# Depthwise 7x7 layer of a four-layer conv kernel: planes in lines of nine values, three window loads per half

## The reference

```python
def _L3_conv_ref(x, w, b):
    xp = jnp.pad(x, ((0, 0), (0, 0), (P, P), (P, P)), mode='reflect')
    out = jax.lax.conv_general_dilated(xp, w, window_strides=(S, S), padding='VALID',
                                       dimension_numbers=('NCHW', 'OIHW', 'NCHW'), feature_group_count=C)
    return out + b[None, :, None, None]
...
x = x + _L3_conv_ref(_gn(x), L3_conv_w, L3_conv_b)
```

## Time and profile before

| | before |
|---|---|
| median of 3 runs | 2541.14 us (2539.9 to 2541.88) |
| the profiled execution's own time | 2520.47 us |
| its span | 2518.7 us |
| mean granted TensorE clock | 0.887 |
| TensorE busy | 1939.4 us (77%) |
| VectorE busy | 1286.7 us (51%) |
| ScalarE busy | 803.1 us (32%) |
| GpSimd busy | 865.8 us (34%) |

### The profile page before, as it was taken

The page is one execution under the profiler, slowest core; times in us unless marked ns, Lnnn a source line. Parts: engine busy times, 40 slices in busy tenths (PEclk is TensorE's granted clock), DMA queues, the critical chain, the costliest instruction groups (busy, mean ns, idle before and its releaser), DMA issues. The chain is left out here.

```text
span 2518.7 us, 36847 instructions
## 1 busy us (share of the span) xinstructions
PE 1939.4 (77%) x15660; PEld 1202.3 (48%) x15660; DVE 1286.7 (51%) x1312; ACT 803.1 (32%) x1265; POOL 865.8 (34%) x452
## 2 busy tenths in 40 slices
PE   2879789868999999999977768777677677774052
PEld 1467666756777777777734322222222222221031
DVE  6345444441111111111171165799999999978803
ACT  2446455540000000000132125633543533335410
POOL 1334333320000000000000040599899899983300
PEclk9899899888999999999988878889889989988555
DMA  5899999976232322221030041778688778863799
GB/s 160 251 325 321 323 298 313 312 230 215 86 93 84 91 86 90 87 88 31 5 97 11 0 138 22 161 196 217 172 212 217 205 178 214 218 175 89 224 216 292
DMA packets 194352, 424.50 MB, mean 169 GB/s; under 512 B 18348, under 2 KB 143276, under 8 KB 183564
## 3 DMA queue, kind: packets, MB, share of 16 engines
q1 hardware_dynamic: 181516, 415.85, 57.9%
q10 hardware_dynamic: 12672, 6.29, 0.9%
HBM read 299.33 MB, written 121.96 MB: 167 GB/s over the span
## 5 line engine op out<-in xcount | busy, mean ns | idle before, releaser
L698 PE MATMUL ps<-mem 128*128 128x288 f16 x5376 | 655.1, 287 | 19.3 <-DMA mem<-depthwise_out 19.3
L698 PEld LDWEIGHTS ps<-mem 128*128 128x128 f16 x5376 | 502.3, 98 | 158.1 <-DMA mem<-depthwise_out 19.6
L1669 POOL TENSOR_TENSOR mem<-mem 128x1024 f32<-128x1024 f32 x192 | 465.8, 2445 | 45.5 <-ACT mem L1603 43.1
L1578 PE MATMUL ps<-mem 128*128 128x512 f32 x768 | 419.7, 679 | 41.2 <-POOL mem L1669 37.5
L1064 POOL TENSOR_TENSOR mem<-mem 128x1536 f16<-128x1536 f32 x16 | 50.8, 3180 | 940.4 <-ACT mem L1042 940.4
L505 PE MATMUL ps<-mem 56*96 56x240 f16 (+1 forms) x5184 | 307.6, 280 | 81.0 <-DMA mem<-base_phases 45.4
L505 PEld LDWEIGHTS ps<-mem 56*96 56x96 f16 x5184 | 297.6, 128 | 105.7 <-DMA mem<-base_phases 50.7
L738 DVE TENSOR_TENSOR mem<-ps,mem 128x128 f16<-128x128 f32 x64 | 18.7, 292 | 591.3 <-ACT mem L759 591.3
L1698 DVE TENSOR_TENSOR_SCAN mem<-mem,ps 128x1024 f32<-128x1024 f32 x132 | 307.8, 2332 | 18.0 <-issue 10.3
L611 DVE TENSOR_TENSOR mem<-ps,mem 96x1024 f16<-96x1024 f32 x144 | 175.5, 1220 | 212.0 <-ACT mem L550 211.9
L1578 PEld LDWEIGHTS ps<-mem 128*128 128x128 f32 x768 | 154.8, 214 | 245.7 <-issue 136.8
(11 more groups left out here) (202 smaller groups left out, 1900.1 us busy)
## 6 DMA issues: line engine op xcount, KB each, us to landing
mem<-l_bc SPq DMA_DIRECT2D x504, 256.0 KB, 4.5
depthwise_out<-mem SPq DMA_DIRECT2D x108, 512.0 KB, 9.0
mem<-depthwise_out SPq DMA_DIRECT2D x32, 1664.0 KB, 10.7
mem<-base_phases SPq DMA_DIRECT2D x72, 448.0 KB
base_phases<-mem SPq DMA_DIRECT2D x56, 512.0 KB, 9.0
mem<-in_wd SPq DMA_DIRECT2D x72, 336.0 KB
mem<-l_planes SPq DMA_DIRECT2D x48, 252.0 KB
mem<-in_x SPq DMA_DIRECT2D x4, 2048.0 KB, 10.7
```

The lines of the kernel that those rows point to most:

```text
L698: ins = nc.tensor.matmul(ps[:, 2 * (i % 2) + h, 0:HALF], d, pw[rows, wa, k, HALF * h:HALF * h + HALF], start=(k == 0 and n == 0), stop=(k ...
L1578: ins = nc.tensor.matmul(py[:, a, :], ident, hh[:, n % 4, 512 * a:512 * a + 512], start=(n % N == 0), stop=(n % N == N - 1))
L1669: nc.gpsimd.tensor_tensor(hh[:, n % 4, :], hh[:, n % 4, :], cs[:, n % 4, :], ALU.mult).then_inc(hc_pool, 1)
```

## The change

A plane now has 18 lines of nine values and two more at the end (164 values). The ninth value of a line stands between the last column of one line and the first of the next, and holds a mirrored neighbour. A shifted plane is therefore the same memory read one value earlier or later, and the six shifted column phases are no longer made: `shift_right` on ScalarE and the left-shifted copy on VectorE are gone. SBUF holds 8 x 4 = 32 planes of a channel. The cast and the subtraction write 8 of 9 values of a line. The mirrored columns are six copies in `pads`, and the mirrored rows are twelve smaller copies in place of six. VectorE clears the whole of both plane buffers once (10,496 words) in place of four strips, and GpSimd clears the window buffer (7,872 words).

In DRAM the planes now lie phase, channel, image. A store of a 128-partition tile writes 4,096 pieces of 656 bytes. A window load takes, for each half, one DMA of 32 phases and two of 12 phases, whose source is read shifted by one value; a partition's row is contiguous over 8 channels and both images (10,496 bytes). That is six DMAs for a batch instead of four.

The windows have memory of their own. The first three batches are loaded as soon as the first two tiles are stored, ahead of tile 2's store in the queue. GpSimd's tap subtraction is cut into twelve pieces of 768 columns, and TensorE waits for taps a part at a time. The matmul reads 8 of each 9 values.

```diff
-PLANE = 18 * 8
+PLANE = 18 * 9 + 2
...
-        planes_d = nc.dram_tensor("l3_planes", [B, C, TAPROWS, 2 * PLANE], F16).ap()
+        planes_d = nc.dram_tensor("l3_planes", [PHASES, C, B, 2 * PLANE], F16).ap()
...
-    pl = ar.take16(2, TAPROWS * 2 * PLANE, dt=F16)
-    cv = pl.rearrange("p a n -> p (a n)").bitcast(F32)[:, 0:NT * HW].rearrange("p (t n) -> p t n", t=NT)
-    pl = pl.rearrange("p a (c r h n) -> p a c r h n", r=4, h=2, n=PLANE)
+    shared = ar.take(NT * HW)
+    cv = shared.rearrange("p (t n) -> p t n", t=NT)
+    pl = shared[:, 0:PHASES * 2 * PLANE].bitcast(F16).rearrange("p (a f r h n) -> p a f r h n", a=2, f=8, r=4, h=2)
...
-        return pl[:, t % 2, 0:8, r, a, 8:136]
+        return pl[:, t % 2, :, r, a, 0:18 * 9].rearrange("p f (y x) -> p f y x", x=9)[:, :, 1:17, 1:9]
...
+    def load_windows(sp, n):
+
+        last = BP * PITCH
+        for t in range(2):
+            c0 = CB * n + BP * t
+            src = planes_d[:, c0:c0 + BP].rearrange("f c b n -> f (c b n)")
+            dst = win[64 * t:64 * t + TAPROWS, n % NW].rearrange("f c n -> f (c n)")
+            sp.dma_start(dst[0:32], src).then_inc(win_in[n % NW], 16)
+            sp.dma_start(dst[32:44, 1:last], src[20:32, 0:last - 1]).then_inc(win_in[n % NW], 16)
+            sp.dma_start(dst[44:56, 0:last - 1], src[0:12, 1:last]).then_inc(win_in[n % NW], 16)
...
                     sp.wait_ge(tap_hi, t + 1)
-                    sp.wait_ge(tap_lo, t + 1)
+                    sp.wait_ge(tap_lo, 3 * (t + 1))
                     load_taps(sp, t + 2)
                 sp.wait_ge(rows_done, t + 1)
                 for p0, b, c0, n in pieces(t):
-                    sp.dma_start(planes_d[b, c0:c0 + n].rearrange("c f n -> c (f n)"),
-                                 pl[p0:p0 + n, t % 2].rearrange("p c r h n -> p (c r h n)")).then_inc(stored[t], 16)
-            sp.wait_ge(tap_hi, NPIECE)
-            sp.wait_ge(tap_lo, NPIECE)
-            sp.wait_ge(stored[0], 16)
-            sp.wait_ge(stored[1], 16)
-            for n in range(NB3):
-                if n >= NW:
-                    sp.wait_ge(conv_sum, n - NW + 1)
+                    sp.dma_start(planes_d[:, c0:c0 + n, b].rearrange("f c n -> c f n"),
+                                 pl[p0:p0 + n, t % 2].rearrange("p f r h n -> p (f r) (h n)")).then_inc(stored[t], 16)
+                if t == 1:
+                    sp.wait_ge(win_cleared, 1)
+                    sp.wait_ge(stored[0], 16)
+                    sp.wait_ge(stored[1], 16)
+                    for n in range(NW):
+                        load_windows(sp, n)
+            for n in range(NW, NB3):
+                sp.wait_ge(conv_sum, n - NW + 1)
                 if CB * n == 128:
                     sp.wait_ge(stored[2], 32)
-                for t in range(2):
-                    for b in range(B):
-                        c0 = CB * n + BP * t
-                        sp.dma_start(win[64 * t:64 * t + TAPROWS, n % NW, :, 2 * PLANE * b:2 * PLANE * b + 2 * PLANE],
-                                     planes_d[b, c0:c0 + BP].rearrange("c f n -> f c n")).then_inc(win_in[n % NW], 16)
+                load_windows(sp, n)
...
-                pe.wait_ge(win_in[n % NW], win_base[n % NW] + 64 * (n // NW + 1))
-                if n == 0:
-                    pe.wait_ge(tap_hi, NPIECE)
-                    pe.wait_ge(tap_lo, NPIECE)
+                pe.wait_ge(win_in[n % NW], win_base[n % NW] + 96 * (n // NW + 1))
+                if n % 3 == 0:
+                    pe.wait_ge(tap_hi, n // 3 + 1)
+                    pe.wait_ge(tap_lo, n + 3)
...
-                                    out = ps[M3 * j:M3 * j + M3, bank(n) + t, 256 * h:256 * h + 256].rearrange("p (b n) -> p b n", b=B)
-                                    ins = nc.tensor.matmul(out, taps_of(n, 4 * h + j, o, t, a), x[:, :, xa, 8 * o:8 * o + 128],
+                                    out = ps[M3 * j:M3 * j + M3, bank(n) + t, 256 * h:256 * h + 256].rearrange("p (b y x) -> p b y x", b=B, x=8)
+                                    ins = nc.tensor.matmul(out, taps_of(n, 4 * h + j, o, t, a), x[:, :, xa, 9 * o:9 * o + 144].rearrange("p b (y x) -> p b y x", x=9)[:, :, :, 1:9],
...
-            def shift_right(t):
-                k = t % 2
-                act.wait_ge(x_lo, 4 * (t + 1))
-                nc.scalar.copy(grid(pl[:, k, 8:11])[:, :, :, 1:8], grid(pl[:, k, 5:8])[:, :, :, 0:7]).then_inc(shifted, 1)
-
             normalise(0)
             taps(0)
             for t in range(NT):
-                shift_right(t)
                 if t + 1 < NT:
                     normalise(t + 1)
                 taps(t + 1)
+            act.wait_ge(x_lo, 4 * NT)
...
-                s = slice(3 * WC * i, 3 * WC * (i + 1))
                 q = slice(0, 64 + TAPROWS)
-                nc.gpsimd.tensor_tensor(wh[q, 1, s], w32[i % 2][q], wh[q, 0, s], ALU.subtract).then_inc(tap_lo, 1)
-
+                for m in range(3):
+                    s = slice(WC * (3 * i + m), WC * (3 * i + m + 1))
+                    nc.gpsimd.tensor_tensor(wh[q, 1, s], w32[i % 2][q, WC * m:WC * m + WC], wh[q, 0, s], ALU.subtract).then_inc(tap_lo, 1)
+
+            nc.gpsimd.memset(win.rearrange("p a c n -> p (a c n)").bitcast(F32), 0.0).then_inc(win_cleared, 1)
...
-            def column(k, c, x):
-
-                return pl[:, k, c].rearrange("p r h (y x) -> p (r h) y x", x=8)[:, :, 1:17, x]
+            def pads(t):
+
+                def at(f, n):
+                    return pl[:, t % 2, f, :, :, n:n + 144].rearrange("p r h (y x) -> p r h y x", x=9)[:, :, :, :, 0]
+
+                for i in (1, 2, 3):
+                    V.tensor_copy(at(8 - i, 9), at(i, 10)).then_inc(columns, 1)
+                for i in (0, 1, 2):
+                    V.tensor_copy(at(i, 18), at(6 - i, 17)).then_inc(columns, 1)
 
             def rows(t):
-                k = t % 2
-                dve.wait_ge(shifted, 2 * (t + 1))
+                p = pl[:, t % 2]
                 dve.wait_ge(columns, 6 * (t + 1))
                 for r in range(1, 4):
-                    V.tensor_copy(pl[:, k, :, r, :, 0:8], pl[:, k, :, 4 - r, :, 8:16])
+                    V.tensor_copy(p[:, 3:8, r, :, 0:9], p[:, 3:8, 4 - r, :, 9:18])
+                    V.tensor_copy(p[:, 0:3, r, :, 1:10], p[:, 0:3, 4 - r, :, 10:19])
                 for r in range(3):
-                    ins = V.tensor_copy(pl[:, k, :, r, :, 136:144], pl[:, k, :, 2 - r, :, 128:136])
+                    V.tensor_copy(p[:, 3:8, r, :, 153:162], p[:, 3:8, 2 - r, :, 144:153])
+                    ins = V.tensor_copy(p[:, 0:3, r, :, 154:163], p[:, 0:3, 2 - r, :, 145:154])
                 ins.then_inc(rows_done, 1)
 
-            for k in range(2):
-                V.memset(pl[:, k, :, 0, :, 0:8], 0.0).then_inc(zeroed, 1)
-                V.memset(pl[:, k, :, 3, :, 136:144], 0.0).then_inc(zeroed, 1)
+            V.memset(shared[:, 0:PHASES * 2 * PLANE], 0.0).then_inc(zeroed, 1)
+            dve.wait_ge(zeroed, 1)
             for t in range(NT):
-                k = t % 2
                 if t == 2:
                     dve.wait_ge(stored[0], 16)
                 for r in range(4):
                     dve.wait_ge(x_norm, 4 * t + r + 1)
-                    V.tensor_copy(main_rows(t, r, 0), phase_rows(r)).then_inc(x_hi, 1)
+                    V.tensor_copy(main_rows(t, r, 0), flat(phase_rows(r))).then_inc(x_hi, 1)
                     dve.wait_ge(x_hi, 4 * t + r + 1)
-                    V.tensor_tensor(main_rows(t, r, 1), phase_rows(r), main_rows(t, r, 0), ALU.subtract).then_inc(x_lo, 1)
+                    V.tensor_tensor(main_rows(t, r, 1), flat(phase_rows(r)), main_rows(t, r, 0), ALU.subtract).then_inc(x_lo, 1)
                 dve.wait_ge(x_lo, 4 * t + 4)
-                V.tensor_copy(grid(pl[:, k, 11:14])[:, :, :, 0:7], grid(pl[:, k, 0:3])[:, :, :, 1:8]).then_inc(shifted, 1)
-                for i in range(3):
-                    V.tensor_copy(column(k, 8 + i, 0), column(k, 3 - i, 0)).then_inc(columns, 1)
-                    V.tensor_copy(column(k, 11 + i, 7), column(k, 6 - i, 7)).then_inc(columns, 1)
+                pads(t)
                 rows(t)
```

More of the change, by code:

```diff
@@ L1747, in layer3 @@
     WC = BP * YS * M3
-    pl = ar.take16(2, TAPROWS * 2 * PLANE, dt=F16)
-    cv = pl.rearrange("p a n -> p (a n)").bitcast(F32)[:, 0:NT * HW].rearrange("p (t n) -> p t n", t=NT)
-    pl = pl.rearrange("p a (c r h n) -> p a c r h n", r=4, h=2, n=PLANE)
+    shared = ar.take(NT * HW)
+    cv = shared.rearrange("p (t n) -> p t n", t=NT)
+    pl = shared[:, 0:PHASES * 2 * PLANE].bitcast(F16).rearrange("p (a f r h n) -> p a f r h n", a=2, f=8, r=4, h=2)
     wh = ar.take16(2, NB3 * WC, dt=F16)
-    at = ar.at
     win = ar.take16(NW, BP, PITCH, dt=F16)
-    end = ar.at
-    ar.at = at
     w32 = [ar.take(3 * WC) for _ in range(2)]
-    ar.at = max(ar.at, end)
-    at = ar.at
     tmp = ar.take(HW)
@@ L1767, in layer3 @@
     tap_lo = sem("l3_taps_low_part")
-    zeroed = sem("l3_unused_borders_cleared")
```

(5 more changed lines are left out.)

## The result

The changed kernel runs in 2538.7 us (median of 20 runs, 2525.8 to 2557.28), the kernel before beside it in 2530.32 us (20 runs, 2522.89 to 2542.49). The ratio is 1.0031 with an interval of 1.0017 to 1.0045. A second comparison of the same two kernels gave 1.0016 (0.9998 to 1.0035). The first interval is clear of no change and the second just touches it. By their middles the loss is 4 to 8 us (0.0016 and 0.0031 of 2530), where I had forecast a gain of 8 us.

A forecast was written before the change was run, and what follows sets the result against it. Layer 3 was taken as bound by planes, window loads and a fixed tail: 2374.5 + 11 + 86.4, plus 7, gave 2479 against 2487.2, so -8 us, 2541.14 becoming 2533; range 2515 to 2561.

The forecast's parts named there:

- I take 7.2, near the middle: Layer 3's window loads: 7.2 us a batch, chosen between 5.4 and 9.3, so 86.4 us for 12 batches.
- strict series: A batch's six window loads one after another, the 12-partition ones at about 82 GB/s: 9.3 us a batch.
- Tile 2's 11 us now lie within it: 9 us net.: Window stream in layer 3: starts 20 us earlier but contains tile 2's 11 us of stores, gaining 9 us net.
- The tail keeps 31.5 us.: End of layer 3, after the last eviction: last store, reading back, adding and storing still take 31.5 us.
- ... so the loads set it.: Layer 3's convolution ends at 2479 us by the window loads; TensorE alone would be through at 2469.
- its present 7.1 us a batch: TensorE's pace in layer 3 before the change, from eviction times: 7.1 us a batch, kept for TensorE alone.
- the memset: VectorE's clear of 10,496 words at layer 3's front: 10.9 us, moving the first cast from 2321.6 to 2330.3.
- the first matmul: Start of TensorE's first batch in layer 3, after its windows land: near 2384 us in the trace.
- the 656 B stores: Plane stores of a 128-partition tile, 2.69 MB in 4,096 pieces: 8.7 to 9.6 us plus about 2, about even.
- rival 4: Shifted destinations or nine-value lines slow DMA or matmuls: 11 us batches end at 2516, 29 us late; chance 0.06.
- The planes: Layer 3's front on VectorE: tiles ready at 2346.3, 2362.3 and 2383.5 us, the front 8 us late.
- Rival 1: Long window rows pay everywhere: 5.4 us a batch, TensorE's pace holds, -20 us to 2521, or 2512 without stops; chance 0.17.

The follow-up runs named there:

- second profile: The changed kernel, unaltered, profiled again in a repeat run: layer 3 took 206.1 us; ratio to the kernel before 1.0016.
- e10: Changed kernel with each 12-partition window load sent to every second partition and tap rows permuted to match: layer 3 191.4 us, ratio to the kernel before 0.9964.
- e4: Changed kernel with the first three batches' window loads issued only after tile 2's stores: layer 3 206.8 us, ratio to the kernel before 1.0043.
- e6: Changed kernel with the two 12-partition window loads made one 24-partition load of the same bytes, without the one-value shift: layer 3 198.1 us.
- e5: Changed kernel without the window loads of batches 3 to 11, whose matmuls reuse the first three batches' data: layer 3 167.3 us.
- e3: Changed kernel with half of VectorE's plane-buffer memset moved to GpSimd: layer 3 211.1 us, ratio to the kernel before 1.0029.

## Why the prediction failed

The sign was wrong: -8 us forecast, +4 to +8 us measured. Set beside the forecast's own times, counted from the start of the layer, the two profiles place the miss:

| us from the layer's start | forecast | after | second profile |
|---|---|---|---|
| third batch starts | 78.8 | 78.9 | 78.8 |
| fourth batch starts | 97.0 | 101.9 | 101.4 |
| last eviction starts | 158.7 | 167.8 | 165.0 |
| end | 191.2 | 207.1 | 206.1 |

(The forecast's column takes 7.2 us a batch, 11 us for tile 2's stores, 2 us for landing and a tail of 31.5 us.) Of the 15.9 and 14.9 us that the end is late, nothing arose in the first three batches, 4.8 and 4.4 us in the hole, 4.2 and 1.9 us in the nine batches behind it, and 6.8 and 8.5 us in the tail.

- **"I take 7.2, near the middle", and the thin loads priced nowhere else.** This is the step that failed: the cost of the 12-partition loads, mis-sized. The sum let them cost a slower batch and nothing more. The batch came out at 7.9 us for the first three, but the stream also started 2.4 us earlier in the layer than forecast, and the two cancelled. What they cost stands behind them. With e10's loads, spread over every second partition and otherwise the same, tile 2's stores land in 19.0 and 19.5 us instead of 29.7 and 29.3, the last eviction starts at +155.2 and +156.4 instead of +167.8 and +165.0, the tail is 35.2 and 31.8 us instead of 38.3 and 40.0, and the layer ends at +191.4 and +189.2: the forecast's own 191.2. So the whole miss goes away with the neighbouring thin loads. I had seen 128, 64 and 56 partitions at 388, 238 and 216 GB/s; I should have let that pattern, and not the hope of overlap, place 12.
  The Trainium skill (SBUF — State Buffer, § Door 1: The DMA port swizzle) has a transfer reach only the ports of the partitions that it touches. These runs agree in direction; my estimate from its figure for the thin loads in strict series, 9.3 us a batch, was too high beside the measured 7.9, and 6.43 and 6.53 in e4.
- **"Tile 2's 11 us now lie within it: 9 us net."** Wrong. The two stores held the queue 18.3 us and the load behind them 10.3 us, and TensorE stood for 19 us. I had costed their bytes and not what is queued ahead of them and behind them on SyncE. e4 gives the worth of the early start: nothing that shows.
- **"The tail keeps 31.5 us."** Wrong: 38.3 and 40.0 us, the largest part of the miss in both profiles. It comes with slower stores of results (11.3 us against 7.7) and a later read back; it is 31.4 us without window loads and 31.8 to 35.2 us with the spread loads, but 40.0 us in e4 and 34.0 in e9, and how the loads lengthen it was not isolated. I had taken it as fixed because its instructions are.
- **"... so the loads set it."** Only in the first half. Behind the hole TensorE waits 5.8 us for windows and 24.3 us for its own instructions, and so it can't be reckoned from a pace of 7.2 or 7.9 us for twelve batches. I had read the stops as a fixed part of "its present 7.1 us a batch" and had not looked at what ends them.
- **Right:** the memset (8.7 us of delay forecast, 8.8 measured); the first matmul (forecast at about +64.7, measured +63.1); 11 to 12.2 us for the 656 B stores (the second measured 12.3); casts, subtractions and 144-matmul batches unchanged (0.69, 1.23 and 4.04 us), so rival 4 fell. The planes were 6.7, 5.7 and 2.9 us late, though, not 8 each: more of the idle time came back than I had counted, although a tap part in three pieces took GpSimd 6.3 to 6.8 us and not 5.2.
- Rival 1 (5.4 us a batch) was wrong as well: with the thin loads spread or joined a batch still takes 6.0 to 6.25 us. And the range's lower end, "rival 1's 2515", is neither of the two times that rival 1 gives, 2521 and 2512.

**Open:** how the neighbouring loads lengthen the tail, why they come 7.9 us apart at the front of the queue and 6.5 us behind tile 2's stores, and why the packets of instructions come late.

## What to carry to other kernels

Loads to few neighbouring partitions were dear here, with rows of 1,312 and of 10,496 bytes alike, and most of their price stood in the transfers behind them: count the partitions of each DMA before its bytes, and spread thin ones over every second partition by permuting the contraction rows. A transfer that is moved ahead of a store is worth only what the queue behind that store leaves of it: work out when the first instruction behind the store is issued. Where TensorE stops with no releaser, look for packets of an instruction queue just before it goes on. When a bound is wide, place the value by the rows' trend, and give the half where the sign turns its full chance.

## What the runs showed of the hardware

- 12 partitions in a neighbouring stretch against 12 with every second one free: 7.9 against 6.25 us for batches of 1.175 MB, two of whose six loads (32 partitions each) are the same; 169 against 208 GB/s. Tile 2's stores, queued behind three such batches, landed in 29.7 us with the neighbours and 19.0 with the spread ones. Behind those stores (e4) the neighbouring loads came 6.43 and 6.53 us apart.
- Destinations shifted by one 2-byte value, and matmuls that read 8 of every 9 values: no cost that shows (6.25 us a batch in e10 against 6.16 and 6.0 in e6; 144 matmuls in 4.04 us before and after).
- With all window traffic gone, TensorE still stopped 20.1 us over nine batches of small matmuls, up to 4.6 us at a time and mostly after 128 matmuls (e5). Each of the 126 such stops in the thirteen traces ends 1.2 to 1.9 us after a 16 KB packet of kind "instruction", one for about 128 matmuls.
- The memset of 10,496 words has a row of 8.80 us on VectorE, with 2.75 us of "issue" ahead of it; half of it had 4.43 and 1.66 us (e3). A forecast from starts, not from the row's duration, came out right: 10.9 us.
